# One-tile experts: whose weights are split first, and z's transposes in one PSUM bank or two

## The reference

```python
x = x + L0_ffn(bi_wkv(x, side, side, w0, u0, cond))      # 4 x 1024 tokens, 1024 channels; ffn: a 1024x1024 linear layer
x = x + L1_ffn(bi_wkv(x, side, side, w1, u1, cond))

def _L1_ffn_ref(x, norm_w, router_w, w1, w2, sg, su, sd):    # E = 32 experts, K = 4 of them per token, I = 512
    residual = x
    h = _rmsnorm(x, norm_w)
    flat = h.reshape(-1, H)
    logits = flat.astype(jnp.float32) @ router_w.T
    scores = jax.nn.softmax(logits, axis=-1)
    topk_w, topk_ids = lax.top_k(scores, K)
    topk_w = topk_w / jnp.sum(topk_w, axis=-1, keepdims=True)
    ...
    gu = lax.ragged_dot(xs, w1, group_sizes)
    g, u = jnp.split(gu, 2, axis=-1)
    act = jax.nn.silu(g) * u
    ys = lax.ragged_dot(act, w2, group_sizes)
    ...
    shared = jax.nn.silu(flat @ sg) * (flat @ su) @ sd
    out = residual + (routed + shared).reshape(B, S, H)
```

## Time and profile before

| | |
|---|---|
| median of 3 runs | 4725.57 us (4722.5 to 4732.86) |
| the profiled execution, its own time | 4722.1 us |
| its span, first to last instruction | 4720.4 us |
| PE busy | 4472.2 us, 95% of the span |
| DVE busy | 2570.2 us, 54% |
| ACT busy | 1794.9 us, 38% |
| POOL busy | 710.3 us, 15% |

### The profile page before, as it was taken

The page is one execution under the profiler, slowest core; times in us unless marked ns, Lnnn a source line. Parts: engine busy times, 40 slices in busy tenths (PEclk is TensorE's granted clock), DMA queues, the critical chain, the costliest instruction groups (busy, mean ns, idle before and its releaser), DMA issues.

```text
span 4720.4 us, 60811 instructions
## 1 busy us (share of the span) xinstructions
PE 4472.2 (95%) x19860; PEld 3543.2 (75%) x19863; DVE 2570.2 (54%) x2765; ACT 1794.9 (38%) x2596; POOL 710.3 (15%) x934
## 2 busy tenths in 40 slices
PE   6667999999999999999999999999999999999998
PEld 2234877768777877878888887887888878888787
DVE  8979999999999653333233434444341143332432
ACT  5655555555555332232222323334331142222321
POOL 1000000000000007211111111111111111111111
PEclk9888999999999999999999999999999999999999
DMA  6664767667676857754354545555553364444543
GB/s 228 236 231 173 278 224 287 241 226 277 234 267 234 277 198 201 248 185 116 78 144 116 161 114 159 169 169 162 167 156 66 62 195 133 108 115 116 160 107 62
DMA packets 247926, 835.07 MB, mean 177 GB/s; under 512 B 28160, under 2 KB 61056, under 8 KB 222976
## 3 DMA queue, kind: packets, MB, share of 16 engines
q1 hardware_dynamic: 172944, 572.77, 34.2%
q0 software_dynamic: 47728, 160.07, 15.8%
q10 hardware_dynamic: 27136, 100.67, 5.7%
HBM read 652.40 MB, written 181.01 MB: 177 GB/s over the span
## 4 chain that ended last, share of the span: by engine, by line
PE 84%; DVE 8%; issue 3%; ACT 3%; DMA 1%; DVEq 0%; ACTq 0%; SPq 0%; POOL 0%; POOLq 0%
PE ps L1544 35%; PE ps L1408 24%; PE ps L1558 17%; PE ps L1477 3%; PE ps L1533 1%; DVE work L932 1%; DVE work L926 1%; PE ps L1430 1%; PE ps L1418 1%; DVE work L953 1%; DVE work L955 1%; DVE work L959 1%; PE ps L1428 1%; DVE work L936 1%; DVE work L1227 1%
## 5 line engine op out<-in xcount | busy, mean ns | idle before, releaser
L1544 PE MATMUL ps<-halves 128*128 128x512 f32 x7152 | 1699.8, 393 | 25.8 <-DVE halves L1303 22.3
L1544 PEld LDWEIGHTS ps<-halves 128*128 128x128 f32 x7152 | 1339.0, 189 | 303.4 <-DVE halves L1303 24.4
L1408 PE MATMUL ps<-halves 128*128 128x512 f32 x6144 | 1451.2, 396 | 22.5 <-issue 22.5
L1408 PEld LDWEIGHTS ps<-halves 128*128 128x128 f32 x6144 | 1154.3, 189 | 296.7 <-issue 59.4
L1558 PE MATMUL ps<-halves 128*128 128x512 f32 x3576 | 834.9, 389 | 1.3 <-DVE halves L1323 1.3
L1558 PEld LDWEIGHTS ps<-halves 128*128 128x128 f32 x3576 | 671.1, 188 | 140.9 <-DVE halves L1323 1.6
L1307 DVE TENSOR_TENSOR halves<-ps,halves 128x1024 fp32r<-128x1024 f32 x150 | 183.7, 1224 | 883.4 <-ACT halves L808 883.4
L1303 DVE TENSOR_TENSOR halves<-work,halves 128x1024 fp32r<-128x1024 f32 (+1 forms) x320 | 440.5, 1433 | 111.8 <-ACT halves L812 111.8
L808 ACT ACTIVATE halves<-ps 128x1024 fp32r<-128x1024 f32 x150 | 154.0, 1027 | 848.9 <-PE ps L1544 848.9
L812 ACT ACTIVATE halves<-work 128x1024 fp32r<-128x1024 f32 (+1 forms) x320 | 369.7, 1220 | 93.7 <-PE ps L1558 66.5
L1323 DVE TENSOR_TENSOR halves<-ps,halves 128x256 fp32r<-128x256 f32 x298 | 112.3, 418 | 494.8 <-ACT halves L840 494.8
(11 more groups left out here) (186 smaller groups left out, 3786.4 us busy)
## 6 DMA issues: line engine op xcount, KB each, us to landing
halves<-split_dram SPq DMA_DIRECT2D x512, 512.0 KB, 5.4
work<-expert_w SPq DMA_DIRECT2D x192, 1024.0 KB, 5.3
split_dram<-halves ACTq DMA_DIRECT2D x32, 1024.0 KB, 4.9
plain<-shared_w SPq DMA_DIRECT2D x32, 512.0 KB, 3.3
gated_dram<-work ACTq DMA_DIRECT2D x32, 512.0 KB, 3.8
work<-side_t ACTq DMA_DIRECT2D x32, 512.0 KB, 5.4
work<-x_t ACTq DMA_DIRECT2D x32, 512.0 KB, 3.4
ratio_dram<-work ACTq DMA_DIRECT2D x32, 512.0 KB, 4.5
```

The lines of the kernel that those rows point to most:

```text
L1408: last = pe.matmul(bank(k % 4), w, op[:, part], start=(c == 0 and w is w_hi and op is hi), stop=(c == CB - 1 and w is w_lo))
L1544: last = pe.matmul(ps_h[:, a * 512:a * 512 + 512], xp[:, xk * P:(xk + 1) * P], wp[:, rhs], start=(xk == 0 and xp is xhi and wp is whi[q]), ...
```

## The change

Two things. First, on ACT and DVE, `expert_loop` becomes `expert_loop_split`: the splitting of the next expert's w1 is moved from the start of the next expert's pass to the end of this one's, and in an expert with a single tile it is written ahead of the splitting of that expert's own w2. The semaphores `w_hi` and `w_lo` are each divided into one for w1 and one for w2, so that the two orders can be counted; SP and PE wait for the new ones at the same places as before. PE's loop and SP's order of loads are as before. Second, z's transposes go to `Z_BANK` and `SUM_BANK` in turn, so that the transposes of block o wait for the copy of block o-2 and not of o-1.

```diff
-PIECES = 10
+W1, W2 = 8, 2
...
+        Z_BANKS = [Z_BANK, SUM_BANK]
...
+        def expert_loop_split(eng, opening, tile, first_weights, second_weights, close):
+
+            eng.wait_ge(s["cols_set"], 1)
+            opening(0)
+            tile(1, 0)
+            end0 = eng.value_load(cuts[0:1, 0:1], min_val=0, max_val=ROUTED_TILES - 2) + 2
+            with eng.If(end0 > 2):
+                with eng.Fori(2, end0) as g:
+                    tile(g, 0)
+            first_weights(1, end0)
+
+            with eng.Fori(1, EXPERTS - 1) as e:
+                first = eng.value_load(cuts[0:1, ds(e - 1, 1)], min_val=0, max_val=ROUTED_TILES - 2) + 2
+                end = eng.value_load(cuts[0:1, ds(e, 1)], min_val=1, max_val=ROUTED_TILES - 2) + 2
+                tile(first, e)
+                with eng.If(first + 1 < end):
+                    second_weights(e, first)
+                    with eng.Fori(first + 1, end) as g:
+                        tile(g, e)
+                    first_weights(e + 1, end)
+                with eng.Else():
+                    first_weights(e + 1, end)
+                    second_weights(e, first)
...
             def load_weights(j):
                 for q in range(GROUPS):
-                    sp.wait_ge(s["w_lo"], (j - 1) * PIECES + (2 * q + 3 if q < 4 else q + 6))
+                    if q < 4:
+                        sp.wait_ge(s["w1_lo"], (j - 1) * W1 + (2 * q + 3))
+                    else:
+                        sp.wait_ge(s["w2_lo"], (j - 1) * W2 + (q - 2))
...
-                sc.activation(ZROWS[:, :, o * P:(o + 1) * P], Z_BANK.rearrange("p (t c) -> p t c", t=HT), ACT.Copy)\
+                sc.activation(ZROWS[:, :, o * P:(o + 1) * P], Z_BANKS[o % 2].rearrange("p (t c) -> p t c", t=HT), ACT.Copy)\
...
-            def head(g, j):
+            def first_weights(j, g):
                 for q in range(4):
                     split_weights(j, q, g)
-                tile(g, j)
+
+            def second_weights(j, g):
                 split_weights(j, 4, g)
                 split_weights(j, 5, g)
...
-            expert_loop(sc, opening, head, tile, close)
+            expert_loop_split(sc, opening, tile, first_weights, second_weights, close)
...
             def square_sums(h, o):
                 pe.wait_ge(s["sq"], h * CB + (o + 1))
                 if o == 0:
-                    wait(pe, "mean", h)
+                    wait(pe, "z_copy", h * CB)
...
-                wait(pe, "z_copy", h * CB + o)
+                wait(pe, "z_copy", h * CB + (o - 1 if o else 0))
...
-                    last = pe.transpose(Z_BANK[:, t * P:(t + 1) * P], Z[o % 2][:, t * P:(t + 1) * P], ident[:, :])
+                    last = pe.transpose(Z_BANKS[o % 2][:, t * P:(t + 1) * P], Z[o % 2][:, t * P:(t + 1) * P], ident[:, :])
```

More of the change, by code:

```diff
@@ L207, in adaln_moe @@
             "a_hi_s a_lo_s o_tr o_copy o_out prep prep_act masks rt rt_act rt_mask rt_pe cnt_copy "
-            "fill_set fill_out add_idx_set apart entry_ready listed_in slots_in cols_set w_hi w_lo w1_read w2_read "
+            "fill_set fill_out add_idx_set apart entry_ready listed_in slots_in cols_set w1_hi w1_lo w2_hi w2_lo w1_read w2_read "
             "rows_in row_idx_set x_tr x_hi x_lo silu_done act_done a_tr a_hi a_lo y_hi y_lo y_out zero_set "
@@ L216, in adaln_moe @@
         ONE_AHEAD = (
-            "o_tr o_copy o_out gated w_lo num ratio ratio_out gated_out a_tr w1_read w2_read act_done x_lo y_lo y_hi"
+            "o_tr o_copy o_out gated w1_lo w2_lo num ratio ratio_out gated_out a_tr w1_read w2_read act_done x_lo y_lo y_hi"
         ).split()
@@ L303, in expert_loop @@
                         tile(g, e)
+            close(eng.value_load(cuts[0:1, EXPERTS - 1:EXPERTS], min_val=1, max_val=ROUTED_TILES - 2) + 1)
+        def expert_loop_split(eng, opening, tile, first_weights, second_weights, close):
[19 more added lines that the diff above has]
+                    second_weights(e, first)
+            last = EXPERTS - 1
+            first = eng.value_load(cuts[0:1, last - 1:last], min_val=0, max_val=ROUTED_TILES - 2) + 2
+            end = eng.value_load(cuts[0:1, last:last + 1], min_val=1, max_val=ROUTED_TILES - 2) + 2
+            tile(first, last)
+            second_weights(last, first)
+            with eng.If(first + 1 < end):
+                with eng.Fori(first + 1, end) as g:
+                    tile(g, last)
             close(eng.value_load(cuts[0:1, EXPERTS - 1:EXPERTS], min_val=1, max_val=ROUTED_TILES - 2) + 1)
@@ L811, in split_part_hi @@
                 sc.wait_ge(w_in[q], (j + 1) * 16)
-                sc.activation(whi[q][:, part], staged(q, part), ACT.Copy).then_inc(s["w_hi"], 1)
+                sc.activation(whi[q][:, part], staged(q, part), ACT.Copy).then_inc(s["w1_hi" if q < 4 else "w2_hi"], 1)
             sc.wait_ge(s["consts_in"], 64)
@@ L1301, in split_part_lo @@
                 part = parts(q)[i]
-                ve.wait_ge(s["w_hi"], j * PIECES + (2 * q + i + 1 if q < 4 else q + 5))
-                ve.tensor_tensor(wlo[q][:, part], staged(q, part), whi[q][:, part].bitcast(f32), ALU.subtract).then_inc(s["w_lo"], 1)
+                if q < 4:
+                    ve.wait_ge(s["w1_hi"], j * W1 + (2 * q + i + 1))
+                else:
+                    ve.wait_ge(s["w2_hi"], j * W2 + (q - 3))
+                ve.tensor_tensor(wlo[q][:, part], staged(q, part), whi[q][:, part].bitcast(f32), ALU.subtract)\
+                    .then_inc(s["w1_lo" if q < 4 else "w2_lo"], 1)
             def split_x(g):
@@ L1356, in close @@
                 weigh(g)
-            expert_loop(ve, opening, head, tile, close)
+            expert_loop_split(ve, opening, tile, first_weights, second_weights, close)
         @block.tensor
@@ L1539, in first_product @@
                     if k % 2 == 0:
-                        pe.wait_ge(s["w_lo"], j * PIECES + (2 * q + k // 2 + 2))
+                        pe.wait_ge(s["w1_lo"], j * W1 + (2 * q + k // 2 + 2))
                     xk = kh * 4 + k
@@ L1551, in second_product @@
                 for q in range(2):
-                    pe.wait_ge(s["w_lo"], j * PIECES + (q + 10))
+                    pe.wait_ge(s["w2_lo"], j * W2 + (q + 2))
                     pe.wait_ge(s["a_lo"], g * 2 + q + 1)
```

## The result

The changed kernel takes 4702.38 us, median of 5 runs (4700.14 to 4706.23), against 4725.57 (4722.5 to 4732.86): 0.9949 of the time before, 95% interval 0.9938 to 0.996. The forecast was 4683 with a range to 4700. It is faster, but by 23 us where 43 were forecast, and the time lies outside the range. The profiled execution took 4706.23 us (span 4704.4), 15.9 less than that of before.

What follows compares the result with a forecast made beforehand. PE was taken to bound the expert phase, with PE and DVE both near full in the first phase. 28.7 us (order of splits) plus 14 us (z) gave 42.7 us gained: 4683 us, range 4668 to 4700.

Steps and rivals of the forecast that it cites:

- What bounds, and what the stop costs: Expert phase: PE is the bound; its stops at four one-tile experts and the slow matmuls behind them cost 30.9 us.
- The four stops: At four one-tile experts PE stands 5.46 us each, waiting for DVE's low parts of the next expert's w1.
- the forecast's 28.7: Net gain claimed from the order of splitting: 30.9 us of stops less 2.2 us of new waits.
- What is late next on DVE: One-tile experts: activation's low part, behind w2 parts, makes PE wait 0.5 to 0.6 us, four times: 2.2 us.
- S: Start of PE's second product (L1558) in the tile before a one-tile expert; times are counted from it.
- The step that failed: One-tile experts: SP's loads of following w2 and w1 come some 8 us later, but are wanted a whole tile later.
- The z stretch: First phase: with two banks a block takes 1.56 instead of 1.83 us; eight stretches gain 14 us, bounds 5 and 18.
- rival 1: First phase: z gain not kept, DVE's scans may set the next start and PE waits longer; 4693 us, chance 14%.
- Rival 2: One-tile experts: new stop replaces the old, from a late `Else` branch or late w2, with half clock; 4699 us, 10%.
- Rival 5: z stretch: taking banks in turn leaves PE at half clock; 33 us slower, 4759; chance 4% with any other loss.

Runs made afterwards that it cites:

- SP's order: Changed kernel, but SP asks for w1 of expert j+1 ahead of w2 of expert j: 4679.56 us, ratio 0.9893; repeated on another chip 4683.1 us, 0.9905.
- POOL's order: Changed kernel, but POOL issues the gather for tile g+3 ahead of the scatter of tile g-1: 4680.74 us, ratio 0.9897; repeat 4807.29 us, 0.9897.
- the order alone: Changed kernel with the new order of weight splits kept, but z's transposes in one bank as before: 4720.05 us, ratio 0.9985.
- z's banks alone: Kernel before plus two banks for z's transposes, with one `expert_loop` and one pair of semaphores as before: 4712.41 us, ratio 0.9963.
- half the bytes: Changed kernel, but from expert 1 each expert load brings only the first 1024 of 2048 columns (wrong weights): 4829.08 us, ratio 0.9943.
- weighing first: Changed kernel, but in one-tile experts ACT and DVE scale the result before ahead of splitting that expert's w2: 4830.67 us, ratio 0.9951.
- both mends: Changed kernel with SP asking for next w1 before this w2, and POOL's gather ahead of the scatter: 4807.5 us, ratio 0.9906.
- tiny loads: Changed kernel, but from expert 1 each expert load brings 128 columns for all 128 partitions (wrong weights): 4810.72 us, ratio 0.9903.

## Why the prediction was wrong

- **What bounds, and what the stop costs.** Right. The four stops and their slow matmuls were worth 30.9 us by the earlier trace rows; with the gather out of the way the expert phase became 28.4 us shorter with SP's order (28.7 by the experts' part alone, and 31.5 and 32.3 with POOL's). That SP's is so near the forecast's 28.7 is in part luck, since the forecast took off 2.2 us for a wait that never came.
- **What is late next on DVE.** Right in kind, and smaller: the forecast had PE wait 0.5 to 0.6 us for L1365. DVE began with w1 at S + 2.81 and not S + 3.60, its two low parts (0.37 us each) were done at S + 17.3 and S + 17.7, and PE came at S + 17.65; no wait is in the trace. The 2.2 us set aside weren't needed.
- **The step that failed.** "SP's loads of the following expert's w2 and w1 come some 8 us later, since SP waits in order for the w2 low parts; they are wanted a whole tile later." The loads are indeed not late for their own use. But held back they go out as a burst, and POOL's scatter and gather, which I costed at nothing, are slow in it. The loads' delay was mis-sized as well: 7.0 us for the first, 0.1 for the last, which is what makes the burst. Beside that, DVE's weighing stands behind the w2 parts too; I named it as queued there and followed it to PE alone, not to POOL, whose gather stands behind the scatter that waits for it. It takes all of these together: with the burst's time taken away, with SP asking earlier, or with the gather ahead of the scatter, the stop is gone or 0.8 us once. Each new stop costs 5.8 us, four of them 23.2: 30.9 - 23.2 = 7.7, and the order alone measured 7.
- **The z stretch.** Right in mechanism, 1.56 us per block, and right in size within what can be told: 14 forecast, 17.5 (11 to 23) measured alone. By the experts' start (their first product after the wait) it is 10.4 us in the profile of the changed kernel and 8.3 to 13.3 in six other profiles with two banks (the rest have the stretch shown at the end of this document), all against 2048.16. On one chip it is 13.7 us: 2037.28 with z's banks alone, 2051.01 with the order alone. Of the 16.3 us that the stretches are shorter, then, some is given back, as rival 1 had it. That it goes into longer waits of PE for DVE isn't shown: the two waits at L1415 and L1471 make 70.1 us in the changed kernel and 65.0 before, but 60.6 with the order alone and 60.5 to 66.9 in the other kernels with two banks.
- **The rivals.** Rival 2 had the form (a new stop in place of the old, with half clock, 4699 us) but another mechanism, late w2 parts or a late branch. That did not happen. With a chance of 10% it was too low for what it stood for: something else late at the same place. Rival 5 fell: half clock lasts 23.7 us over the eight stretches, and 24.4 before. What the Trainium skill tells of cycling PSUM banks (the page named in the prediction) is not borne out here.

What stays open is why a scatter's first packet comes 5 us after its issue in a burst, why the stretches' 16.3 us aren't all kept, and why a load of half the bytes but as many packets, each shorter, helps by 0.7 us of landing at most.

## What to carry to other kernels

Where an edit lets a queue in order wait longer, price two things: when its transfers are wanted, and what else they hit when they then come all at once. Follow each late result to every engine that waits for it, the software queue included, to the next thing behind that. When a stop of known price is removed and most of it comes back one tile later, look first for a transfer whose order of request no longer fits the order in which its space comes free.

## What the runs showed that was not expected

- A gather that lands in 4.1 us takes 11.6 when it stands behind a scatter and both share the engines with six loads of 1 MB.
- Loads of 64 partitions instead of 128 kept the DMA engines as full (share 0.98), at 201 GB/s instead of 361.
- A 0.18 us copy on POOL took 4.10 us, and the issue of a scatter 4.92 instead of 1.59, beside DVE operations with both operands in SBUF.
- A 4 KB packet of the scatter takes 327 ns and one of the gather 159, beside a burst or without.
- In five of the profiles (half the bytes, weighing first, both mends, tiny loads, POOL's order again) one stretch of the first phase takes some 130 us longer. In that of half the bytes:

```profile
1775.00:1915.00 140.00, 38.88 (x77) 20.78 (x77) 6.89 (x11) 6.74 (x10) 90.16 (x94) 0.51 0.13 38
```

  PE does 77 matmuls there in 140 us, over long pieces one every 2.8 us, and waits for nothing that the profile shows (60 waits by issue over the run, 124.9 us). In the changed kernel's profile the same window has 591, at 136.80 us busy and clock 0.99. What causes it is open.
